# A gated two-layer kernel: the order of transpositions, context loads, table factors and weight loads in its first phase

## What is computed

```python
x = x + tanh(g_xattn[0]) * einsum('emk,enk->emn', quant_fp8_1x128(LN(x)), quant_fp8_128x128(ctx))
x = x + tanh(g_ffn[0])   * (quant_int8(rms_norm(LN(x)) * gamma) @ ternary(W0).T) * w_scale
x = x + tanh(g_xattn[1]) * softmax_attention(q=LN(x), k=ctx, v=ctx)      # heads of 128 rows
x = x + tanh(g_ffn[1])   * top2_of_8_experts(LN(x), router_w, Wa, Wb)
```

## Time and profile before

| what | value |
|---|---|
| median of 3 runs | 2086.92 us |
| the profiled execution | 2083.42 us |
| its span, first to last instruction | 2081.6 us |
| PE busy over the span | 1865.1 us (90%) |
| DVE busy | 1540.6 us (74%) |
| ACT busy | 1264.9 us (61%) |
| POOL busy | 775.3 us (37%) |
| mean granted TensorE clock | 0.976 |

### The profile page before, as it was taken

How to read it: one execution, slowest core, us unless ns; L and a number is a source line. 1 busy time by engine, 2 the same in 40 slices (tenths; PEclk the granted TensorE clock), 3 DMA queues, 4 the chain that set the end, 5 groups by cost and what they waited for, 6 DMA issues and landing times.

```text
span 2081.6 us, 26392 instructions
## 1 busy us (share of the span) xinstructions
PE 1865.1 (90%) x8968; PEld 839.6 (40%) x8968; DVE 1540.6 (74%) x2383; ACT 1264.9 (61%) x2043; POOL 775.3 (37%) x1101
## 2 busy tenths in 40 slices
PE   1698999874689999999999999999999999999987
PEld 0244444331234444444444444444444444444433
DVE  7899899984577777777777777777777777777651
ACT  4688888762455655556556565556656656565650
POOL 3555565322233333333333333333333333333320
PEclk9999999997789999999999999999999999999999
DMA  9667776884578878877887878887888887887771
GB/s 202 162 180 193 217 198 184 241 199 132 111 137 168 166 159 162 164 159 153 164 167 160 165 164 160 163 166 154 162 166 163 167 162 157 163 171 157 133 151 41
DMA packets 923735, 340.49 MB, mean 164 GB/s; under 512 B 849617, under 2 KB 898769, under 8 KB 923601
## 3 DMA queue, kind: packets, MB, share of 16 engines
q1 hardware_dynamic: 923600, 338.81, 76.8%
HBM read 93.36 MB, written 33.55 MB: 61 GB/s over the span
## 4 chain that ended last, share of the span: by engine, by line
DVE 25%; ACT 19%; issue 18%; POOL 10%; PE 7%; DMA 5%; SPq 0%; POOLq 0%; ACTq 0%; DVEq 0%
ACT slot L799 9%; DVE tiny L1401 8%; POOL tiny L646 5%; ACT arena L791 5%; DVE tiny L1073 4%; POOL tiny L644 4%; DVE slot L1405 3%; ACT tiny L785 3%; DMA probs<-slot 2%; DMA slot<-slot 2%; DVE arena L1413 2%; DVE slot L1388 2%; ACT slot L813 2%; PE sc L911 1%; PE accs L997 1%
## 5 line engine op out<-in xcount | busy, mean ns | idle before, releaser
L1405 DVE SCALAR_TENSOR_TENSOR slot<-arena,tiny,slot 128x1024 f16<-128x1024 f32 x256 | 328.4, 1283 | 315.6 <-ACT slot L799 315.5
L969 PE MATMUL sc<-arena,slot 128*128 128x512 f16 x1536 | 376.9, 386 | 34.7 <-ACT arena L791 25.0
L799 ACT ACTIVATE slot<-arena,tiny 128x1024 f16<-128x1024 f32 x256 | 293.8, 1147 | 178.7 <-POOL tiny L646 164.4
L644 POOL TENSOR_SCALAR tiny<-tiny 128x1 f32<-128x1 f32 x256 | 98.9, 386 | 698.7 <-ACT arena L791 698.7
L1401 DVE TENSOR_REDUCE tiny<-sc 128x1 f32<-128x1024 f32 x256 | 306.2, 1206 | 14.5 <-PE sc L969 14.2
L791 ACT ACTIVATE arena<-sc,tiny,head_tab 128x1024 f32<-128x1024 f32 x256 | 308.2, 1204 | 8.6
L785 ACT ACTIVATE tiny<-tiny,head_tab 128x1 f32<-128x1 f32 x256 | 73.9, 289 | 350.9 <-DVE tiny L1401 350.9
L969 PEld LDWEIGHTS sc<-arena,slot 128*128 128x128 f16 x1536 | 151.1, 99 | 224.2 <-ACT arena L791 32.4
L985 PE MATMUL accs<-probs,arena 128*128 128x512 f16 x512 | 194.5, 380 | 12.7 <-issue 12.3
L952 PE MATMUL accs<-wb_hi,slot 128*128 128x512 f16 x512 | 195.0, 381 | 8.5 <-DMA slot<-slot 8.5
L911 PE MATMUL sc<-probs,slot 128*128 128x512 f16 x768 | 174.4, 387 | 25.3 <-DMA slot<-slot 25.0
(11 more groups left out here) (211 smaller groups left out, 2896.8 us busy)
## 6 DMA issues: line engine op xcount, KB each, us to landing
arena<-in_x SPq DMA_DIRECT2D x32, 512.0 KB, 4.8
x_scratch<-arena SPq DMA_DIRECT2D x32, 512.0 KB, 3.1
slot<-x_scratch SPq DMA_DIRECT2D x32, 512.0 KB, 4.1
slot<-in_ctx SPq DMA_DIRECT2D x32, 512.0 KB, 4.2
out<-arena SPq DMA_DIRECT2D x32, 512.0 KB, 3.4
slot<-in_L_ffn_Wa SPq DMA_DIRECT2D x12, 512.0 KB, 4.8
slot<-in_L_ffn_Wb SPq DMA_DIRECT2D x12, 512.0 KB, 6.2
wb_hi<-in_ctx SPq DMA_DIRECT2D x64, 64.0 KB, 2.4
```

The costliest lines, as they stand in the source:

```text
L799: act.activation(PH[c % 2], PF[c % 2], ACT.Identity, scale=rinv[c % 2][:]).then_inc(s_ph.sem, 1)
L969: mm = pe.matmul(sc[:, c % 2, h * HALF:(h + 1) * HALF], q[i][:, c * P:(c + 1) * P], k[j][:, h * HALF:(h + 1) * HALF], start=start, stop=stop)
L1405: dve.scalar_tensor_tensor(out=PL[c % 2], in0=PF[c % 2], scalar=rinv[c % 2][:], in1=PH[c % 2], op0=ALU.mult, op1=ALU.subtract).then_inc(s_ ...
```

## The change

It edits only the first phase:

- SP: `turn_x(j + 1)` stands ahead of the context and statistics loads of a step instead of behind them. The four transposes of tiles 0 and 1, which stood ahead of the loop, are issued in step -5, between the loads of chunks 14 and 15 and that of chunk 16.
- SP, from step 25: the transposition of ternary slice r is issued a step later (`turn_w0(j - 25)`) and behind the step's `load_prep`; slices 2 to 7 are loaded in step r + 23. Slice 5's ternary part lies in `slot[4]`, and it waits for x1 tile 26 instead of 27.
- POOL: from step 23 the low part of x is made a step later, at the head of the step, and from step 25 it waits for `w_lo_set` of slice j - 25.
- DVE: `c_factors` ends with the rounding factor; the rest is `c_diagonals`, a step later, behind `c_add`. For the first batch it stands behind the first chunk's `c_add`. The maxima of chunks 8 to 15 stand in other steps.
- PE and ACT: for the first batch the second half of a chunk is filled into the two other PSUM banks (those of `SQ`), so it need not wait for the eviction of the first half.

```diff
+X_TURN_FROM = -5
-PREP_TILES = (25, 26, 27)
+PREP_TILES = (25, 26)
...
-            return [m for m in range(PER_BATCH, TILES) if j == (m - C_MAX + 1 if m < 2 * PER_BATCH else m - C_MAX)]
+            return [m for m in range(PER_BATCH, TILES) if j == (min(m - 17, m // 2 - 11) if m < 2 * PER_BATCH else m - C_MAX)]
...
-            for n in range(X_EARLY):
-                turn_x(n)
             for j in range(FIRST, LAST + 1):
                 if is_x(j + 5) and j + 5 > 3:
                     load_x(j + 5)
+                if j == X_TURN_FROM:
+                    for n in range(X_EARLY):
+                        turn_x(n)
+                if is_x(j + 1) and j + 1 >= X_EARLY:
+                    turn_x(j + 1)
                 if is_c(j + C_MAX + 1, C_RING):
                     load_c(j + C_MAX + 1)
                 for t in stats_of(j + 1):
                     load_stat(t)
-                if is_x(j + 1) and j + 1 >= X_EARLY:
-                    turn_x(j + 1)
-                if PREP <= j < PREP + KB:
-                    turn_w0(j - PREP)
+                for r in range(KB):
+                    if j == PREP - (2 if r < 2 else 1) + r:
+                        load_prep(r)
+                if PREP < j <= PREP + KB:
+                    turn_w0(j - PREP - 1)
                 if is_x(j - 1):
                     store_x1(j - 1)
...
-                for r in range(KB):
-                    late = 1 if r % 2 and r > KB // 2 else 2
-                    if j == PREP - late + r:
-                        load_prep(r)
...
+                elif is_x(j + 1) and j >= PREP - 1:
+                    after(pool, w_lo_set, j - PREP - 1)
+                    x_low(j + 1)
...
                     x_round(j + 2)
-                    x_low(j + 2)
+                    if j < PREP - 2:
+                        x_low(j + 2)
...
-                    after(pe, c_out, m - 1)
+                    after(pe, c_out, m - 1, 1 if b == 0 else 2)
...
+                elif b == 0:
+                    after(pe, c_out, m - 1)
                 else:
                     pe.wait_ge(c_out.sem, c_out.at(m, 1))
...
+                if j == FIRST + 1 or j - 1 in TABLE_STEPS:
+                    c_diagonals((j - 1 + C_ABS) // PER_BATCH)
```

More of the change, by code:

```diff
@@ L145, in flamingo_two_layers @@
         RAW_EARLY = [rings[1][:, 2], rings[1][:, 3], rings[2][:, 2]]
-        RAW_LATE = [XP[tile % X_RING] for tile in PREP_TILES]
+        RAW_LATE = [slot[4][:]] + [XP[tile % X_RING] for tile in PREP_TILES]
         def raw(kind, r):
@@ L214, in flamingo_two_layers @@
         fills, SQ = (accs[:, i:i + 2, :].rearrange("p a n -> p (a n)") for i in (0, 2))
-        filled = fills.rearrange("p (r t n) -> p t n r", r=HALF_CHUNK, t=2)
+        fill_in = {0: [fills, SQ], 1: [fills, fills]}
+        filled = {w: [f.rearrange("p (r t n) -> p t n r", r=HALF_CHUNK, t=2) for f in fill_in[w]] for w in fill_in}
         w_out = [w.rearrange("p t k (s r) -> p t (k s) r", s=GROUPS) for w in w_both]
@@ L601, in _ @@
                     c_tables(0)
-                if j in TABLE_STEPS:
-                    c_tables((j + C_ABS) // PER_BATCH)
+                if j - 1 in TABLE_STEPS:
+                    c_tables((j - 1 + C_ABS) // PER_BATCH)
                 if j == PREP - 1:
@@ L718, in c_evict @@
                 r = i * CHUNK + half * HALF_CHUNK
-                act.activation(w_out[b % 2][:, :, :, r:r + HALF_CHUNK], filled, ACT.Identity, scale=1.0 / FILL)\
-                   .then_inc(c_out.sem, 1)
+                act.activation(w_out[b % 2][:, :, :, r:r + HALF_CHUNK], filled[min(b, 1)][half], ACT.Identity,
+                               scale=1.0 / FILL).then_inc(c_out.sem, 1)
             def x1_square(n):
@@ L883, in fill @@
                 b, i = divmod(m, PER_BATCH)
+                at = fill_in[min(b, 1)][half]
                 if half == 0:
                     pe.wait_ge(c_q.sem, c_q.at(m))
-                    after(pe, c_out, m - 1)
+                    after(pe, c_out, m - 1, 1 if b == 0 else 2)
                     if i == 0:
@@ L898, in fill @@
                     r = half * HALF_CHUNK + i
-                    mm = pe.matmul(fills[:, 2 * i * P:2 * (i + 1) * P], CQ[m % 2][:, r * P:(r + 1) * P], diag[:, b % 2, :],
+                    mm = pe.matmul(at[:, 2 * i * P:2 * (i + 1) * P], CQ[m % 2][:, r * P:(r + 1) * P], diag[:, b % 2, :],
                                    start=True, stop=True)
@@ L1169, in c_factors @@
                 dve.wait_ge(cf_spread.sem, cf_spread.at(b))
-                after(dve, cf_tab, b - 1)
                 dve.tensor_reduce(csafe.rearrange("p (n k) -> p n k", k=KB),
@@ L1182, in c_factors, with c_diagonals @@
                 dve.tensor_scalar(cstep[:, i:i + 1], crec[:], FP8_MAX * STEP_FP8, None, ALU.mult).then_inc(cf_k.sem, 1)
+            def c_diagonals(b):
+                i = b % 2
+                after(dve, cf_tab, b - 1)
                 dve.tensor_reduce(cham[:], csafe.rearrange("p (n k) -> p n k", k=KB), AX.X, ALU.max).then_inc(cf_d.sem, 1)
```

## The result

The changed kernel takes 2116.86 us (median of 4 runs, 2112.16 to 2117.73) against 2085.12 us (median of 4, 2083.06 to 2087.57) for the kernel before: a ratio of 1.0144 (95% interval 1.013 to 1.0158), 1.4% slower. The sign is as forecast and the size is not: the forecast was 2104, its range ended at 2113. The profiled execution took 2116.71 us, with a span of 2114.8 us against 2081.6.

The account below looks back on a forecast made before the run. DVE was taken to bound the middle, a chain through several engines the weights stage. Profiled 2083.4 + 3.5 (start, middle adding nothing) + 14 (weights) = 2100.9, about 2104 us on the median's scale; range 2081 to 2113.

Parts of the forecast that it names:

- The middle: Steps 1 to 22: the round stays near 13 us per step and adds nothing; +3.5 us stands at step 22.
- The check named for the middle: A shorter step between 237 and 376 us would refute that DVE sets the pace of steps 1 to 22.
- DVE's 93%: Steps 1 to 22: DVE's work fills 93% of a step of about 13 us and sets its length.
- The start: Up to the first product: later transpositions cost +2.9 us at chunk 16 and +0.9 behind the diagonals, +3.8 together.
- +3.5 that I carried to step 22: Delay followed from +3.8 us at the first product, near 0 in step 6, to +3.5 from step 15 on.
- The stage of the weights: Slices 0 to 7 and tile 31: slices follow at 16.65 us against 12.6; the last `finish_x1` starts +14 us later.
- the -1.7: Forecast change in us from tile 22's `finish_x1` to slice 0's low parts, with `x_safe` no longer slowed by POOL.
- The ring's fixed terms: Per-slice chain of waits through DVE, POOL and SP: 1.90 + 2.61 + 3.1 + 0.3 for signals = 7.95 us.
- L: Time from a slice's first weight load's issue to the ternary transposition's landing: between 4.75 and 9.4 us, taken as 8.7.
- the tail: From slice 6's low parts to the last `finish_x1`: only DVE's own work is left, 7.5 us against 16.4 before.
- The rival in which the transposition overtakes the loads: Weight slices: the transposition does not wait for the loads, 12.7 us per slice, total 2081 us; chance 0.16.

Follow-up runs that it names:

- early store: Changed kernel with the store of x1 between `turn_x` and the context load, up to step 23; 2097.91 us, ratio 1.0056 to the kernel before.
- `turn_x` undone: Changed kernel with `turn_x(j + 1)` put back behind the context and statistics loads; 2104.44 us, ratio 1.0083 to the kernel before.
- ternary part first: Changed kernel with the transposition of ternary slice r ahead of the three weight loads of slice r + 2; 2094.05 us, ratio 1.003 to the kernel before.
- no POOL wait: Changed kernel without POOL's wait for `w_lo_set` ahead of `x_low` from step 25 on; 2097.27 us, ratio 1.0054 to the kernel before.

## Why the prediction was right and wrong

**The step that failed: "SP's round holds the same instructions as before ... so the round stays near 13 us per step, and only its phase turns. The middle adds nothing."** The instructions were the same. The round is closed by something that is no instruction: the landing of its last one. I had put that landing into the sum as a remainder and kept it, 2.6 us, while the change altered what the store is queued behind. It became 5.0 in the steps with a statistics load, and the middle lost 14.8 us where I gave it nothing. The two runs on this part leave no other explanation of that size: counted at tile 22, undoing the order takes 12.0 us back, moving the store alone takes 20.9.

It is the same effect that I did price at the end, a DMA landing later because of the loads issued just ahead of it: 3.0 against 7.5 us for transpositions. A single load of 512 KB was enough for it. I applied it to the transposition, which the diff named, and not to the store, whose line did not change. The check named for the middle, a shorter step, also looked only one way.

**The claim that DVE's 93% sets the middle was also too strong.** It holds from tile 14 on, where all six kernels take 90.3 us to tile 22. Before that it does not: from 160 to 280 us DVE is busy 93% of the time in the kernel before, 83% in the changed one and 97% with the early store. A share of 93% says that at most 7% can be gained; it does not say that nothing can be lost. The row that I took it from, 237 to 376.5 us, lies for the most part behind the steps with context loads, and the average step in it is 11.8 us (tiles 11 to 22), not 13.

**The start.** Forecast +3.8 at the first product, measured 86.75 against 84.49, +2.3, and +1.1 at tile 0's `finish_x1`. The views, DVE's wait for chunk 16 and SP's queue ahead of it:

```profile
69.30 1.22 DVE L1166 TENSOR_REDUCE slot<-wb_hi 128x1 f32<-128x1024 f32 x1 [6.06 <-DMA wb_hi<-in_ctx]
```

```profile
43.85 12.74 SPq L319 DMA_DIRECT2D tern<-in_ctx  x16
56.70 5.49 SPq L394 DMA_TRANSPOSE slot<-slot  x4
62.24 15.69 SPq L307 DMA_DIRECT2D wb_hi<-in_ctx  x24
```

The shape is as forecast, a wait of 6.06 where it was 0.61. The size was not: the pairs were through at 56.6 and not 57.4, the four transposes took 5.49 and not 6.3, and chunk 16 came 1.0 us late, not 2.9. The other 1.2 arises between there and tile 3's statistics, which came at 82.17 against 79.92. It is one operation of the diagonals, on 128x1 elements, that now runs beside POOL's rounding of a chunk (79.00 to 81.12) and took 0.16 us before:

```profile
79.72 1.41 DVE L1203 SCALAR_TENSOR_TENSOR tiny<-tiny 128x1 f32<-128x1 f32 x1
```

It takes 1.41 us in all five traces with this code. The start as a whole is soft: the four experiments share its code, and their first products came at 86.9, 86.5, 91.0 and 85.9 us, so 1.4 to 6.5 us late, with my +3.8 inside.

The experiment with `turn_x` undone comes out at +3.9 at tile 22, close to the +3.5 that I carried to step 22 through the tables. That agreement is in part luck: it covers a start that was smaller (tile 0 at +2.3 there) and 1.6 us in the middle that I did not trace.

**The stage of the weights** was right in mechanism and size. `x_safe` took 0.23 us (the -1.7 measured -1.6). The ring's fixed terms were forecast 7.95 and measured 16.06 - 8.23 = 7.83; L was forecast 8.7 and measured 435.79 - 427.56 = 8.23. Six rounds took 97.8 us against 99.9, the tail 7.3 against 7.5. The rival in which the transposition overtakes the loads fell: 6.4 us from issue to landing, above the 5.9 - 1.75 = 4.15 at which the ring would not have mattered. That nothing orders DMAs across the 16 engines, which the Trainium skill says ("DMA: Bandwidth & Descriptors", section "Two DMAs through the same engine are not ordered"), did not bring the landing forward here.

**The weighing of a page's sentence.** I took the row, eight issues in 5.06 us, over the sentence of the Trainium skill ("DMA: Bandwidth & Descriptors", section "Issuing engines are not separate DMA queues") that initiating a DMA is usually a small time beside the DMA. For 64 KB pieces the changed kernel shows the same, eight issues in 5.17 us. The start came out between the two, so it does not decide for either.

**The second phase** took 5.5 us more in the profiled executions, for the same instructions. In windows of the two traces laid from the last `finish_x1` on, the granted clock is lower in two places. The kernel before, its stretches from 540 and from 1700 us:

```profile
540.00:800.00 260.00, 236.10 (x1118) 104.17 (x1118) 185.34 (x250) 152.70 (x218) 89.50 (x153) 0.95 0.78 151
...
1700.00:2081.60 381.60, 351.86 (x1715) 157.72 (x1713) 245.01 (x352) 198.10 (x282) 116.10 (x208) 0.99 0.71 141
```

and the changed one, 27.6 us later:

```profile
567.60:827.60 260.00, 237.44 (x1119) 104.58 (x1120) 185.03 (x250) 152.46 (x218) 89.74 (x154) 0.93 0.78 151
...
1727.60:2114.80 387.20, 358.92 (x1723) 159.94 (x1721) 246.41 (x352) 198.75 (x283) 116.10 (x208) 0.97 0.70 140
```

In the other kernels this part of the span took 1602.7 (`turn_x` behind), 1597.8 (store early), 1603.3 (ternary part first) and 1600.2 (no POOL wait). I gave it no spread at all in the range. It is worth up to 6 us from one execution to another, and alone it would have moved the forecast's 2113 edge. Whether the first phase's shape sets it, or chance, these runs don't tell.

**The sum.** The measured time is 12.9 us above the forecast of 2104. The middle gave +15.1, the second phase +5.5, the start -2.7 and the stage of the weights -2.1. Another -3.4 is scale: I added the 3.5 us by which the kernel before's profiled execution lay under its median, and the changed kernel's lay 0.15 under; rounding is the rest. So the middle alone is more than the whole miss, and what else was off nearly cancelled by luck.

## What to carry to other kernels

In a loop that a queue closes, write down what its first instruction waits for, and ask for each move what is now queued directly ahead of *that* transfer: moving one step past another also changes the landing of a third whose line never changed. Before a new wait or a new order, walk once round every closed chain through it and add it up. Here six rounds of the one that was walked came out within 3%, and the one that was taken as unchanged cost 14.8 us. And look at what stands there by size: behind eight small loads the store landed as early as before, behind one large load it did not.

A late landing that no ring closes over costs little, so a ring can be opened at its cheapest place.

## What the runs showed of the hardware that was not expected

A store of 512 KB lands 3.2 us after its issue behind a pair of transposes (median of nine, 160 to 280 us of the kernel before). Issued right behind eight context loads of 64 KB it lands after 2.9 to 3.0 us. Issued right behind a statistics load of 512 KB it lands after 4.8 to 6.3 us, whether context loads stand ahead of that or not. In the three kernels with this order, 100 to 280 us, this holds for all 9 stores of the first kind and all 30 of the second. With the pair of transposes between it and the loads, or ahead of the loads (3.1 us at the median with the early store), it is quick in most steps (single stores 2.6 to 4.9 us). No run moved the statistics load alone.

A DVE operation on 128x1 elements took 1.41 us beside POOL's rounding of a chunk, and 0.16 without (at 72.56 us of the kernel before). A stretch of this kind was foreseen, at 0.8 us, and was larger.
